# Rotary attention of layer 0: one score bank a head, peaks found with one wide maximum, output projection spread over four steps

## What is computed

```python
Q = (x @ W_q).reshape(b, s, N_HEADS, HEAD_DIM).transpose(0, 2, 1, 3)      # 16 heads of 32
K = (x @ W_k).reshape(b, s, N_KV_HEADS, HEAD_DIM).transpose(0, 2, 1, 3)   # 4 key heads
Qr = _apply_rope(Q, positions)
K_rep = jnp.tile(K, (1, rep, 1, 1)); V_rep = jnp.tile(V, (1, rep, 1, 1))
Kr = _apply_rope(K_rep, positions)
scores = jnp.einsum('bhqd,bhkd->bhqk', Qr, Kr) / HEAD_DIM ** 0.5
weights = jax.nn.softmax(scores, axis=-1)
out = jnp.einsum('bhqk,bhkd->bhqd', weights, V_rep)
out = out.transpose(0, 2, 1, 3).reshape(b, s, d)
return out @ W_o
```

## Time and profile before

| | us |
|---|---|
| median of three runs | 2746.16 |
| the profiled execution's own time | 2746.78 |
| its span | 2745.0 |
| TensorE busy in the span | 2525.7 (92%) |
| VectorE busy | 1754.8 (64%) |
| ScalarE busy | 1081.3 (39%) |
| GpSimd busy | 1023.4 (37%) |
| peaks on TensorE, L599, 512 matmuls | 216.4 |
| maxima on VectorE, L692, 512 reductions | 326.3 |
| scores, L612, 512 matmuls | 148.2 |
| exponentials, L750, 256 of 1024 columns | 250.1 |
| pairs on GpSimd, L539, 128 | 301.7 |
| first score to last values of the stage | 177.0 to 735 |

### The profile page before, as it was taken

How to read it: one execution, slowest core, us unless ns; L and a number is a source line. 1 busy time by engine, 2 the same in 40 slices (tenths; PEclk the granted TensorE clock), 3 DMA queues, 4 the chain that set the end, 5 groups by cost and what they waited for, 6 DMA issues and landing times. The chain is left out here.

```text
span 2745.0 us, 35908 instructions
## 1 busy us (share of the span) xinstructions
PE 2525.7 (92%) x12212; PEld 1711.3 (62%) x12212; DVE 1754.8 (64%) x4115; ACT 1081.3 (39%) x2569; POOL 1023.4 (37%) x756
## 2 busy tenths in 40 slices
PE   7889899898769999999697999969999979999998
PEld 3334344343258888888575777756777656667886
DVE  6467667585335555555646999947999823335886
ACT  2225445353422333222214777725767721111111
POOL 2418757575711111110004676624444410001442
PEclk9979999999989999999899999999999999999999
DMA  7651302120020000000212101010000078882101
GB/s 226 209 130 24 66 12 55 24 55 1 16 92 16 15 30 15 15 0 1 93 43 74 51 21 32 21 39 23 14 5 15 1 270 294 296 296 88 57 24 62
DMA packets 167335, 193.64 MB, mean 71 GB/s; under 512 B 51982, under 2 KB 114446, under 8 KB 166784
## 3 DMA queue, kind: packets, MB, share of 16 engines
q1 hardware_dynamic: 155648, 178.90, 20.9%
q0 software_dynamic: 11520, 12.64, 1.5%
HBM read 161.95 MB, written 54.53 MB: 79 GB/s over the span
## 5 line engine op out<-in xcount | busy, mean ns | idle before, releaser
L692 DVE TENSOR_REDUCE mx<-bank 128x1 f32<-128x512 f32 x512 | 326.3, 678 | 123.9 <-PE bank L599 119.3
L539 POOL TENSOR_TENSOR probs<-probs 128x1024 f32<-128x1024 f32 x128 | 301.7, 2378 | 211.8 <-PE bank L622 165.7
L750 ACT ACTIVATE probs<-bank 128x1024 f32<-128x1024 f32 x256 | 250.1, 1023 | 274.0 <-PE bank L612 274.0
L1546 POOL TENSOR_SCALAR mix<-mix,sm 128x256 f32<-128x256 f32 (+1 forms) x256 | 232.6, 920 | 175.2 <-DVE sm L1443 174.8
L1486 ACT ACTIVATE ms<-ms,sm 128x256 f32<-128x256 f32 (+1 forms) x512 | 247.6, 486 | 94.1 <-DVE sm L1414 93.2
L599 PE MATMUL bank<-k_parts,q_parts 96*128 96x512 f32 x512 | 216.4, 474 | 10.1 <-DVE mx L692 4.7
L599 PEld LDWEIGHTS bank<-k_parts,q_parts 96*128 96x128 f32 x512 | 93.5, 195 | 170.8 <-DVE mx L692 138.9
L926 POOL TENSOR_TENSOR up_lo<-up_raw,up_hi 128x1024 fp32r<-128x1024 f32 x16 | 46.1, 2902 | 402.3 <-ACT up_hi L916 402.3
L1414 DVE CUSTOM_DVE_ANT_0 ms<-bank,misc 128x256 f32<-128x256 f32 (+1 forms) x512 | 184.7, 399 | 2.4
L612 PE MATMUL bank<-q_parts,k_parts 97*128 97x512 f32 x512 | 148.2, 405 | 15.4 <-ACT probs L750 8.9
L996 DVE TENSOR_TENSOR hid<-bank,sg 128x512 f32<-128x512 f32 x64 | 44.2, 691 | 180.4 <-ACT sg L946 180.4
(11 more groups left out here) (227 smaller groups left out, 5873.0 us busy)
## 6 DMA issues: line engine op xcount, KB each, us to landing
ewg<-in_L_ffn_Wg_dram SPq DMA_DIRECT2D x32, 704.0 KB, 6.8
ewu<-in_L_ffn_Wu_dram SPq DMA_DIRECT2D x32, 704.0 KB, 8.0
ewd<-in_L_ffn_Wd_dram SPq DMA_DIRECT2D x32, 512.0 KB, 5.2
q_parts<-qk_dram SPq DMA_DIRECT2D x48, 256.0 KB, 4.5
up_raw<-in_L_ffn_W_dram SPq DMA_DIRECT2D x16, 512.0 KB, 4.4
ewd<-in_L_ffn_Wd_dram SPq DMA_DIRECT2D x32, 192.0 KB, 5.4
qk_dram<-qk_hi SPq DMA_DIRECT2D x4, 1280.0 KB, 5.5
qk_dram<-qk_lo SPq DMA_DIRECT2D x4, 1280.0 KB, 8.0
```

Source lines behind the costliest of these rows:

```text
L539: pool.tensor_tensor(probs[:, even, half, :], probs[:, even, half, :], probs[:, odd, half, :], ALU.add).then_inc(S["paired"], 1)
L692: dve.reduce_max(mx[:, U % 2, q, h:h + 1], bank[:, h, :], AX.X).then_inc(S["max"], 1)
L750: act.activation(probs[:, s % BUFS, 2 * x:2 * x + 2, :], bank[:, 2 + 2 * x:4 + 2 * x, :], ACT.Exp, scale=scale).then_inc(S["exps"], 1)
L1546: pool.tensor_scalar(mix[:, p % 2, h, 0:w], mix[:, p % 2, h, 0:w], sm[:, p % 3, 8 + h:9 + h], None, ALU.mult).then_inc(S["probs"], 1)
```

## The change

- A slot's two peaks go to one pair of banks, 0 and 1 or 2 and 3 in turn. VectorE takes both in one reduction over 1024 columns that also negates and writes `neg` directly; `mx` and the `negate` instruction are gone. At each head's first slot it now waits for the DMAs that read the place in `neg` before.
- Scores use banks 4 and 5 in turn, one head each. ScalarE makes one exponential of 512 columns a head, four a step instead of two; a score waits for the exponential of two heads earlier.
- TensorE's order within a step is now: score 0, peaks, score 1, values, score 2, score 3, sums (odd steps), peaks.
- The projection's four groups stand in steps 2 to 5, one a step, behind score 1, all into bank 0. In these steps both slots' peaks stand at the end, behind the wait for the addition. The last chunk's four groups go to four banks with no wait between.

```diff
-                def peak(U, q, h, after_y=None):
...
-                    wait(pe, S["max"], n - 1)
-                    pe.matmul(bank[:, h, :], qp[0:R, u, q * P:(q + 1) * P],
-                              kp[0:R, b, u % KV0, h * CH:(h + 1) * CH], start=True, stop=True).then_inc(S["peaks"], 1)
...
+                def peaks(n):
...
+                    wait(pe, S["max"], n - 1)
+                    for h in range(2):
+                        mm = pe.matmul(bank[:, 2 * (n % 2) + h, :], qp[0:R, u, q * P:(q + 1) * P],
+                                       kp[0:R, b, u % KV0, h * CH:(h + 1) * CH], start=True, stop=True)
+                    mm.then_inc(S["peaks"], 1)
+
+                def score(V, s, j):
+
+                    b, U = V // (TURNS // BATCH), HPT * V + j
+                    wait(pe, S["exps"], HPT * (V * QB + s) + j - 1)
+                    if s == 0:
+                        wait(pe, S[f"shift{j}"], 64 * (V + 1))
+                    pe.matmul(bank[:, 4 + j % 2, :], kp[0:R + 1, b, U % KV0, s * P:(s + 1) * P],
+                              qp[0:R + 1, U % UN0, :], start=True, stop=True).then_inc(S["scored"], 1)
...
-                        if cc and V % QT0 == 1 and s % 4 == 0:
-                            for half in range(2):
-                                project(cc - 1, s // 2 + half, min(2 * U * SUBS, 2 * HEADS * SUBS))
-                            after_y = (cc - 1) * SUBS + s // 2
-                        peak(U, q, 0, after_y)
-                        peak(U, q, 1, after_y)
+                        projects = cc and V % QT0 == 1 and 2 <= s < 2 + SUBS
                         score(V, s, 0)
+                        if not projects:
+                            peaks(n)
                         score(V, s, 1)
-                        peak(U, q + 1, 0)
-                        peak(U, q + 1, 1)
-                        if s or V:
-                            values(*last)
-                        N = (V * QB + s) // 2 - 1
-                        if s % 2 and N >= 0:
-                            sums(N)
+                        if projects:
+                            wait(pe, S["max"], min(n, SLOTS0) - 1)
+                            project(cc - 1, s - 2, 0)
+                        if N:
+                            values((N - 1) // QB, (N - 1) % QB)
+                        score(V, s, 2)
+                        score(V, s, 3)
+                        if s % 2 and N > 1:
+                            sums(N // 2 - 1)
+                        if projects:
+                            wait(pe, S["added"], (cc - 1) * SUBS + s - 1)
+                            peaks(n)
+                        peaks(n + 1)
...
-                    dve.reduce_max(mx[:, U % 2, q, h:h + 1], bank[:, h, :], AX.X).then_inc(S["max"], 1)
...
+                    if q == 0:
+                        wait(dve, S[f"shift{U % HPT}"], 64 * (U // HPT))
+                    wait(dve, S["peaks"], n + 1)
+                    dve.tensor_reduce(neg[:, U % HPT, q:q + 1], bank[:, 2 * (n % 2):2 * (n % 2) + 2, :], AX.XY, ALU.max,
+                                      negate=True).then_inc(S["max"], 1)
...
+                    wait(act, S["scored"], HPT * (V * QB + s) + j + 1)
...
+                    act.activation(probs[:, s % BUFS, j, :], bank[:, 4 + j % 2, :], ACT.Exp,
```

More of the change, by code:

```diff
@@ L521, in _ @@
                     if U % HPT == 0 and V >= 0 and V + QT0 < TURNS:
-                        wait(sp, S["scored"], (V + 1) * 2 * QB)
+                        wait(sp, S["scored"], (V + 1) * EXPS0)
                         queries((V + QT0) // QT0, V % QT0)
@@ L536, in pair @@
                         half = slice(2 * x, 2 * x + 2)
-                        wait(pool, S["exps"], 2 * (V * QB + s) + x + 1)
+                        wait(pool, S["exps"], HPT * (V * QB + s) + 2 * x + 2)
                         wait(pool, S["valued"], V * QB + s)
@@ L595, in peak @@
                             wait(pe, S[f"k_loaded{b}"], 48)
-                    if after_y is not None:
-                        wait(pe, S["added"], after_y + h + 1)
                     wait(pe, S["max"], n - 1)
-                    pe.matmul(bank[:, h, :], qp[0:R, u, q * P:(q + 1) * P],
-                              kp[0:R, b, u % KV0, h * CH:(h + 1) * CH], start=True, stop=True).then_inc(S["peaks"], 1)
[L602 to L614, removed]
+                    for h in range(2):
[9 more added lines that the diff above has]
+                              qp[0:R + 1, U % UN0, :], start=True, stop=True).then_inc(S["scored"], 1)
                 def values(V, s):
                     b = V // (TURNS // BATCH)
-                    wait(pe, S["exps"], 2 * (V * QB + s) + 2)
+                    wait(pe, S["exps"], HPT * (V * QB + s + 1))
                     if s == 0:
@@ L710, in invert, with add @@
                         inv.then_inc(S["rec"], 1)
-                def add(cc, q):
+                def add(cc, q, to):
                     wait(dve, S["y"], cc * SUBS + q + 1)
                     row = X[:, cc * SUBS + q, :]
-                    dve.tensor_tensor(row, row, bank[:, q % 2, :], ALU.add).then_inc(S["added"], 1)
-                for U in range(LEAD):
-                    for q in range(SUBS):
-                        maximum(U, q, 0)
-                        maximum(U, q, 1)
-                    negate(U)
+                    dve.tensor_tensor(row, row, bank[:, to, :], ALU.add).then_inc(S["added"], 1)
+                for n in range(LEAD * SUBS):
+                    maximum(n)
                 for V in range(TURNS):
@@ L724, in _ @@
                     for s in range(QB):
-                        U, q = HPT * V + LEAD + s // 2, s % 2 * 2
-                        if cc and V % QT0 == 1 and s % 4 == 0:
-                            for half in range(2):
-                                add(cc - 1, s // 2 + half)
-                        maximum(U, q, 0)
-                        maximum(U, q, 1)
+                        n = 2 * (V * QB + s) + LEAD * SUBS
+                        if cc and V % QT0 == 1 and 2 <= s < 2 + SUBS:
+                            add(cc - 1, s - 2, 0)
+                        maximum(n)
                         if V and 3 <= s < 3 + SUBS:
                             invert(V - 1, s - 3)
-                        maximum(U, q + 1, 0)
-                        maximum(U, q + 1, 1)
-                        if s % 2 == 1:
-                            negate(U)
+                        maximum(n + 1)
                 for part in range(SUBS):
@@ L776, in _ @@
                             take_sums(V - 1)
-                        exponent(V, s, 1)
+                        exponent(V, s, 2)
+                        exponent(V, s, 3)
                 take_values(TURNS - 1)
```

76 lines of the change are left out of this document (33 added, 43 removed).

## The result

The changed kernel took a median of 2718.19 us (2717.15 to 2719.21, four runs), beside it the kernel before 2745.36 us (2743.39 to 2746.52). The ratio is 0.9902, its 95% interval 0.9885 to 0.9919: 27 us, one per cent faster. The prediction was 2721 us. The profiled execution took 2717.67 us, with a span of 2715.9.

The account below looks back on a forecast made before the run. TensorE was taken as the bound, its waits worth only 0.65 us a pair of steps. Ordinary turns −2, projection −24.5, start +1.5 and tail 0 gave −25 from 2746.8, median 2721 us; own range 2711 to 2731.

Parts of the forecast that it names:

- The budget: Ordinary turns: TensorE's waits worth 0.65 us a pair of steps, new order takes 0.59 back; turn 30.42 against 30.57.
- The second strip change: Odd steps, sums now alone between full-width matmuls: pair of steps without waits 0.34 us longer.
- The score wait: Even steps: next step's score 0 waits 0.14 us for an exponential, plus 0.1 without its load ahead; 0.25 us.
- The wide maximum: VectorE's reduction over 1024 columns: 1.21 us, bounds 0.68 and 1.36; covered, no wait left on it in ordinary steps.
- The round trip of a score bank: Score start through its exponential to the bank's next score: 0.54, 0.60 and 0.05, together 1.19 us.
- The projection: Projecting turns: norm 3 us early, its wait and slow clock gone; 16 us a case, three 48 against 72.5, −24.5 us.
- The start: Stage start: score 0 queued behind VectorE's reductions that wait for head 0's DMA; +1.5 us, bounds 0 and +5.
- The tail: Turn 15: sums wait for GpSimd, whose work is unchanged; 0 us, between −1 and +2.
- A: Score 0 behind even steps, then score 1: score round trip decides; at 1.9 us, 2760 us; chance 0.07.
- B: Changes between 32-column strips and full width on TensorE cost nothing; 18 us less, 2703 us; chance 0.08.
- C: Projecting turns: norm later than 12.5 us, so the projection's wait survives; 19 us, 2741 us; chance 0.05.
- D: TensorE's clock falls from more but shorter waits; a tenth of the stage at 1.2 GHz loses 28 us, 2750; chance 0.03.

Follow-up runs that it names:

- the first two experiments: Old projection placement put back in the changed kernel: 2739.9 us, ratio 0.9981; new placement alone in the kernel before: 2725.79 us, ratio 0.9933.
- the first profile of before: The kernel before, unchanged, in its first profiled execution: 2746.8 us, span 2745.0.
- the second: The kernel before, unchanged, run once more for another profile: 2744.49 us, one run.

## Why the prediction held

Step by step, with what was measured beside what was said:

- *The budget.* All waits of TensorE were said to be worth 0.65 us a pair of steps, and the new order to take 0.59 of it back: a turn of 30.42. Measured 30.38 to 30.45. Shown by the trace and, part by part, by the experiments. The second strip change, said 0.34: with the peaks last, odd steps take 4.29 to 4.32 with it and 3.94 to 3.96 without. The score wait, said 0.25: a pair takes 3.2 + 4.37 = 7.6 in the changed kernel and 3.03 + 4.32 = 7.35 with the peaks last.
- *The wide maximum.* 1.21 said, 1.213 measured, with no wait on it in ordinary steps. Its gain was said to be bounded by TensorE's waits, and it was: an ordinary turn got 0.1 to 0.2 us shorter, where VectorE saves 0.14 us a slot.
- *The round trip of a score bank.* 1.19 said from four rows, 1.19 measured, twice.
- *The projection.* Said 16 us a case and turns 4 and 5 near 77; measured 77.0, of which 60.8 are two ordinary turns: 16.2. The margin of the norm was said to be 3 us and is 2.9. What a case takes beyond two ordinary turns fell from 24.2 us to 16.2, 23.8 in all where 24.5 were said. (The prediction's 7.13 / 2 is 3.57 and not 3.43; the 3.43 that its sum uses is right, since it is eight starts 0.43 apart.) The pieces hold too: the steps of groups 2 to 4 are 0.72, 0.64 and 0.72 us over their work, 2.1 together for 1.9 said, and step 6 of the projecting turn takes 4.16 us, 0.9 over an ordinary even step for 0.8 said. Most of it is the placement, by the first two experiments: of the 24.6 us by which the three pairs of turns got shorter, the new placement alone takes 21.1, and putting the old one back loses 19.9.
- *The start.* +1.5 said; step 1 stands at 186.12 against 184.15, +2.0, and turn 1 starts 2.0 us later than in the first profile of before, 1.2 later than in the second. The mechanism was as described (VectorE waits 16.22 us in front of head 4's first maximum), the first score 1 us later than I had it.
- *The tail.* 0 said, and it is 0 by luck, from two parts that were not in the sum. Turn 14, in which the peaks end, takes 29.16 us instead of 27.71, +1.4. Turn 15, to its last values, is unchanged at 25.8. Behind it the last sums, which wait for GpSimd's last pair, stand 3.6 us behind the last values instead of 4.95: 1.3 back.
- *The median.* 25 us said, 27.2 measured, with an interval of about 4.6 us either way. The stage's own gain by the traces is 23.3 or 24.4, as above. The remaining 3 to 4 us of the median lie where no instruction changed; they are within the interval and within the 5 us by which two executions of one kernel differ behind the stage.

The rivals: A (the score round trip) needed 1.65 us and found 1.19. The old order with the new banks shows what the same round trip costs where the scores stand together: 77 us slower than the kernel before. B (strip changes cost nothing, the rule of hidden weight loads in the Trainium skill, "TensorE: Matmul & The Clock Gate", section "Step-by-step: what each phase is for") is out for these changes of width: behind sums as behind values the full-width matmul stands 0.34 from its successor instead of 0.235, and a pair with one change more is longer. C did not occur, with 2.9 us to spare. D did not occur in the changed kernel, whose granted clock is 1.00 from turn 1 to the last values, but see the last section.

## What to carry to other kernels

Before costing a faster instruction, add up the waiting engine's work from starts in the timeline, without its waits: the difference to the measured period is all that any such edit can give, and an order that adds a switch or a short wait can spend it. Where a long wait for a slow chain stands at a fixed place in a full queue, moving the consumer by a step or two of other work can be worth more than any instruction. A cost taken away may bring out a wait that stood behind it: the sums beside the values showed 1 us alone, and 15 once the peaks at the end had covered that wait.

## What the runs showed of the hardware

- **The clock fell with no wait longer than 0.54 us before it.** In the kernel with the old order and new banks, in step 1 of turn 2, TensorE waited 0.54 us in front of the four scores and 0.20 inside them, after 0.45 in step 0. Then values and sums took nearly twice their time, for one step:

```profile
266.78 0.98 PE L608 MATMUL bank<-q_parts,k_parts 97*128 97x512 f32 x2 [0.54 <-ACT probs L734]
267.97 0.98 PE L608 MATMUL bank<-q_parts,k_parts 97*128 97x512 f32 x2 [0.20 <-ACT probs L734]
268.79 0.72 PE L598 MATMUL bank<-k_parts,q_parts 96*128 96x512 f32 x2
269.44 1.94 PE L617 MATMUL bank<-probs,v 128*32 128x512 f32 x8
271.15 1.76 PE L628 MATMUL bank<-probs,misc 128*32 128x512 f32 x8
```

  The granted clock over 250 to 310 us is 0.94, so some 7 of these microseconds ran at 1.2 GHz. Five ordinary turns (1, 2, 3, 7 and 12) have such a step 1, of 6.58 to 6.64 us where the others have 5.00, and so have the three projecting turns (5, 9 and 13), of 6.04 to 6.06. The waits are not enough by themselves: turn 10 has the same ones at the same places, and its values and sums run at full speed.

```profile
596.36 0.98 PE L608 MATMUL bank<-q_parts,k_parts 97*128 97x512 f32 x2 [0.54 <-ACT probs L734]
597.55 0.98 PE L608 MATMUL bank<-q_parts,k_parts 97*128 97x512 f32 x2 [0.20 <-ACT probs L734]
598.37 0.62 PE L598 MATMUL bank<-k_parts,q_parts 96*128 96x512 f32 x2
598.93 1.06 PE L617 MATMUL bank<-probs,v 128*32 128x512 f32 x8
599.81 1.04 PE L628 MATMUL bank<-probs,misc 128*32 128x512 f32 x8
```

  The same holds of turns 4, 6, 8, 11 and 14. What else decides is not shown. This is the behaviour of rival D. The Trainium skill ("TensorE: Matmul & The Clock Gate", section "A second HAM failure mode: psum-queue depth-cycling") describes it, and these eight falls behind short waits agree with it. In the other kernels of this case the granted clock stays at 1.00 from turn 1 to the last values but for two places: behind the long wait of the projection's old place, and once in turn 15 of the old kernel with the new placement. There it fell at 700.6 us, behind waits of 0.97, 0.91 and 1.32 us; the kernel before has waits of 0.97, 0.90 and 1.31 us at the same places and kept its clock.
- A full-width matmul that a semaphore has just released costs the next one 0.1 us (0.34 instead of 0.235 from start to start, 251.66 to 252.00 in the trace with the sums beside the values), just as one behind a strip does. A wait of 0.14 us so costs 0.25.
- One reduction over two PSUM banks took 1.213 us for 1024 columns, where 512 took 0.678. The second 512 columns so cost 0.535, whatever the crossing from one bank to the next costs included.
